# A layer with attention and experts on one core: six of nine DMA pieces of zeros in the early batch, not three, and behind the first raw weight chunk

## The reference

```python
x = x + cross_attention(_layernorm(x), ctx_768, ...)   # 16 heads of 64, its own layer norms on x and context
x = x + self_attention(_layernorm(x), W_qkv, W_o)      # 16 heads of 32, q = k = v
x = x + moe(_layernorm(x), ...)                        # 8 experts of 512 x 2048 x 512, top 2 of 8
...
logits = (x @ gate_w + gate_b) / TEMP
topk_vals, topk_idx = jax.lax.top_k(logits, TOP_K)
masked = jnp.where(keep, logits, -jnp.inf)
gate_probs = jax.nn.softmax(masked, axis=-1)
h = jax.nn.gelu(jnp.einsum('bsd,edf->bsef', x, w1) + b1, approximate=False)
expert_out = jnp.einsum('bsef,efd->bsed', h, w2) + b2
out = jnp.einsum('bse,bsed->bsd', gate_probs, expert_out)   # then a layer norm with ln_g, ln_b
```

## Time and profile before

| what | value |
|---|---|
| median of 3 runs | 1472.52 us (1472.13 to 1472.53) |
| profiled execution, its own time | 1469.05 us |
| its span, first to last instruction | 1467.4 us |
| mean granted clock of TensorE | 0.985 |
| PE busy | 1382.4 us, 94% |
| DVE, ACT, POOL busy | 53%, 40%, 11% |
| DMA | 207.52 MB, mean 141 GB/s |

### The profile page before, as it was taken

How to read it: one execution, slowest core, us unless ns; L and a number is a source line. 1 busy time by engine, 2 the same in 40 slices (tenths; PEclk the granted TensorE clock), 3 DMA queues, 4 the chain that set the end, 5 groups by cost and what they waited for, 6 DMA issues and landing times.

```text
span 1467.4 us, 24647 instructions
## 1 busy us (share of the span) xinstructions
PE 1382.4 (94%) x8042; PEld 879.9 (60%) x8043; DVE 781.0 (53%) x1871; ACT 586.5 (40%) x1082; POOL 156.8 (11%) x200
## 2 busy tenths in 40 slices
PE   6879999999999999999996899999999999999997
PEld 5658677686676876768764544444444444444442
DVE  5665876868777777787665532222222222232225
ACT  3565665756747567466670211212112121121100
POOL 1001012020020200302003100000000000000005
PEclk9999999999999999999999999999999999999997
DMA  9793142341322412325028807524325166100005
GB/s 363 269 351 144 52 154 92 116 161 50 134 102 104 182 50 109 127 79 209 29 91 329 320 28 279 217 83 158 135 105 196 44 256 249 44 21 21 14 15 172
DMA packets 53568, 207.52 MB, mean 141 GB/s; under 512 B 4902, under 2 KB 5012, under 8 KB 47388
## 3 DMA queue, kind: packets, MB, share of 16 engines
q1 hardware_dynamic: 40320, 123.14, 22.7%
q0 software_dynamic: 13184, 83.89, 14.9%
q10 hardware_dynamic: 28, 0.01, 0.0%
HBM read 144.11 MB, written 62.91 MB: 141 GB/s over the span
## 4 chain that ended last, share of the span: by engine, by line
PE 80%; DVE 8%; ACT 4%; issue 4%; POOL 2%; DMA 1%; SPq 0%; DVEq 0%; ACTq 0%; POOLq 0%
PE bank L624 22%; PE bank L1466 8%; PE bank L1424 7%; PE bank L606 6%; PE bank L608 5%; PE bank L607 5%; PE bank L1387 4%; PE bank L1492 4%; PE bank L1408 3%; PE bank L616 3%; PE bank L1433 2%; PE bank L1448 2%; PE bank L1514 2%; ACT moe_w L954 2%; DVE moe_w L1115 2%
## 5 line engine op out<-in xcount | busy, mean ns | idle before, releaser
L624 PE MATMUL bank<-moe_w,arena 128*128 x736 | 330.9, 592 | 0.0
L492 DVE SCALAR_TENSOR_TENSOR arena<-bank,now_scales,arena 128x512 f32<-128x512 f32 x92 | 69.1, 751 | 344.0 <-PE bank L608 344.0
L624 PEld LDWEIGHTS bank<-moe_w,arena 128*128 128x128 f32 x736 | 132.7, 190 | 132.5 <-issue 132.5
L1424 PE MATMUL bank<-moe_w 128*128 128x257 f32 x768 | 189.8, 385 | 6.5 <-DVE moe_w L886 6.5
L429 ACT ACTIVATE arena<-arena 128x512 f32<-128x512 f32 x92 | 58.3, 633 | 335.7 <-DVE arena L492 335.7
L1424 PEld LDWEIGHTS bank<-moe_w 128*128 128x128 f32 x768 | 138.2, 192 | 25.6 <-DVE moe_w L886 5.8
L606 PE MATMUL bank<-moe_w,arena 128*128 x368 | 139.7, 379 | 1.3 <-POOL pool_mark L384 1.3
L607 PE MATMUL bank<-moe_w,arena 128*128 x368 | 139.5, 379 | 0.0
L608 PE MATMUL bank<-moe_w,arena 128*128 x368 | 139.5, 379 | 0.0
L1466 PE MATMUL bank<-moe_w 128*128 128x512 f16 x384 | 114.4, 379 | 10.0 <-ACT moe_w L943 7.0
L929 ACT ACTIVATE moe_w<-bank,cols,ugain 128x512 f32<-128x512 f32 x96 | 74.6, 777 | 61.6 <-PE bank L1467 60.8
(11 more groups left out here) (234 smaller groups left out, 2158.4 us busy)
## 6 DMA issues: line engine op xcount, KB each, us to landing
moe_w<-w_halves POOLq DMA_DIRECT2D x8, 4096.0 KB, 13.2
moe_w<-in_L_ffn_w_dram POOLq DMA_DIRECT2D x8, 4096.0 KB, 24.4
w_halves<-moe_w SPq DMA_DIRECT2D x48, 512.0 KB, 3.1
xs_rows<-blocks SPq DMA_DIRECT2D x8, 2048.0 KB, 14.8
moe_w<-in_L_ffn_w_dram SPq DMA_DIRECT2D x16, 1024.0 KB, 6.3
arena<-in_ctx_dram SPq DMA_DIRECT2D x32, 384.0 KB
arena<-in_L_ffn_w_dram SPq DMA_DIRECT2D x8, 1024.0 KB, 4.8
blocks<-in_L_ffn_w_dram SPq DMA_DIRECT2D x8, 1024.0 KB, 4.8
```

Source lines behind the costliest of these rows:

```text
L492: nc.vector.scalar_tensor_tensor(out=h_sb[:, fb % 2, :], in0=bank[fb % 2][:, :], scalar=now_scales[:, KD:KD + 1], in1=b1_rows[:, bass.ds(s ...
L624: last = nc.tensor.matmul(Y[:, :], hT_sb[:, fb % 2, c, :], moe_flat[:, bass.ds((e % 2) * 16384 + 8192 + (4 * fb + c) * DIM, DIM)], start=( ...
L1424: last = nc.tensor.matmul(bank[h][:, 0:KEYS], qkT[:, c, b, h * P:(h + 1) * P], cnT[:, b % 2, c, :], start=(c == 0), stop=(c == KC - 1))
```

## The change

The early batch has six zeros instead of three, and the raw chunk 0 is issued ahead of it. Group 0 is handed the zeros that remain: three, all behind the first context piece. The other engines' programs are the same.

```diff
-ZERO_FIRST = 3
+ZERO_FIRST = 6
@@ in SP's program
+            sp.wait_ge(setup_full, 8)
+            raw_load(0, 0)
             sp.wait_ge(zeros_ok, 1)
             for e in range(ZERO_FIRST):
                 zero_rows(e)
-            sp.wait_ge(setup_full, 8)
-            raw_load(0, 0)
             group(0, True, range(ZERO_FIRST, EXPERTS + 1))
```

## The result

| | before | changed |
|---|---|---|
| median of 6 runs each | 1471.74 us (1469.27 to 1472.53) | 1463.83 us (1462.10 to 1465.97) |
| ratio, 95% interval | | 0.9951 (0.9939 to 0.9964) |
| profiled execution (span) | 1469.05 us (1467.4) | 1463.71 us (1462.1) |
| start of L1480 to the next group's first L1387 | 23.58 us | 17.31 us |

The changed kernel is 7.2 us faster by the ratio (5.3 to 9.0); 6.0 was forecast, and a median of 1466.5 us. The profiled execution was forecast at 1463.05 and took 1463.71. The last line of the table takes the stage round the moved wait by itself, from 97.58 to 121.16 before and from 97.22 to 114.53 after: 6.27 us less.

A forecast was written before the change was run, and what follows sets the result against it. PE, 94% busy, could gain only from idle and low clock, here its wait for the third context piece at group 0's end: 5.1 + 0.9 = 6.0 us, profiled execution 1463.05, median 1466.5 us, range 1463.0 to 1470.0.

The forecast's parts named there:

- (a): Raw chunk 0 issued ahead of the zeros: no engine waits for it, so landing earlier is worth 0 us.
- (b): Three more zeros in the early batch fill the DMA idle from 55.8 to 64.8; the sixth lands at 71.3.
- (c): First context piece, queued behind six zeros, lands at 72.1, 1.7 us before DVE's read; loss 0 to 0.4 us.
- (d): Third context piece is issued at 88.1, lands by 93.3, before DVE wants it at 96.35; 6.09 us idle goes.
- The 1.26 us of cover: First context piece's lateness hidden from PE: L1107 ends at 77.10 and PE wants its result at 78.36.
- The lower bandwidth: At 358 GB/s a 2 MiB zero takes 5.9 us; first piece 2.0 late, 0.7 lost, gain 5.3 not 6.0.
- (e): End of group 0: ACT's second row sum limits next, idle 0.30; L962 and L1492 5.1 us earlier, not 6.1.
- (f): L1492 regains 2.6 us of low clock, less 1.7 for one 3.4 us stretch: 0.9 us, bounds 0 and 2.6.
- the two outcomes: Clock falls once behind PE's remaining idle (0.9 us regained), or is spared (2.6; total 7.7, 1464.8 us, within forecast's range).
- the rival of the clock that takes back: Later 1.2 GHz stretches, up to 1.7 us each, take the gain back: 1470.8 us; chance 0.09.
- The third piece wasn't late: Rival: third context piece late all the same, SP held until 92, PE's wait stays: 1472.5 us; chance 0.07.
- The slower side: Rival: first context piece starves DVE; at 8 us per zero, 5.4 us slower, 1477.9 us; chance 0.06.

## Why the prediction was right

**(a) The chunk.** Worth 0 us, as forecast: the chunk alone gave 0.9998, and six zeros without it all of the gain.

**(b), (c), (d) The queue.** SP was free for the first piece as forecast and issued the third with its m_full. The step that was mis-sized is in (c): the first piece lands "0.8 later" than the sixth zero, at 72.1, with 1.7 to spare. In the profile it was there at 73.78, 1.2 behind the sixth zero, which itself took 6.2 us instead of 5.13 and landed at 72.6. These 1.7 us are all that was to spare. In five profiles of kernels with six early zeros DVE waited 0, 0.35, 1.86, 1.97 and 2.58 us, of which 0, 0, 0.56, 0.68 and 1.28 reached PE. The forecast's bounds of 0 and 0.4 were too narrow. The sum lacked one thing more: the time at which DVE wants the piece was read from a single execution. In the three profiles that have two stretches of low clock ahead of 60 us (the kernel before and both of the changed kernel) DVE is ready for the piece at 73.4 to 74.2; in the nine without them at 71.9 to 72.6. The waits of 1.86, 1.97 and 2.58 all belong to the nine, those of 0 and 0.35 to the three. The piece itself was there at 73.8 to 74.6 in the four profiles in which DVE waited. That the changed kernel's own profiles show next to no wait is thus partly luck. The 1.26 us of cover was right (1.30).

**The lower bandwidth.** The Trainium skill, "DMA: Bandwidth & Descriptors", Specifications, has about 358 GB/s as one core's share of the HBM. The trace does not agree: this core moved 409 GB/s over 9 us of zeros. The piece was 1.86 to 2.58 late in three profiles, but not by slower zeros: where it was 2.58 late, the six zeros landed 5.1 to 5.2 us apart.

**(e) The next wait.** Right to the tenth: ACT's idle fell to 0.30, L1500 came 2.35 after L962 and L1492 4.51 after it. Reckoned from the start of L1480, L1492 comes 8.64 after it instead of 13.72: 5.08 us, forecast 5.1.

**(f) The clock.** One stretch of 3.41 us, as taken. It gave back 1.19 us, not 0.9: at full clock L1492 has 6.98 us from its start to the next group, not 7.4. The 7.4 doubled the listed length of half of it in group 1 (3.69), and a listed length reaches past the start of the next group of matmuls: 32 in one piece are listed with 7.14, and the next group starts 6.98 after them. The clock part of the wait was thus 2.88, measured by itself with PE filled, of which the change got 1.19 and the low stretch kept 1.69 (1.7 forecast). 5.08+1.19 is the 6.27 of the stage. That the forecast took the right one of the two outcomes is luck: behind the same two idles of PE the clock fell in four profiles and didn't in three, and 1.7 us hang on it.

**The sum.** 6.3 us at the stage, 5.3 at the end of the two profiled executions, 7.2 (5.3 to 9.0) in the runs. The 1.0 between stage and end of the profiles: this start was 0.4 us earlier, and 1.3 us were lost behind the stage (1346.2 us from L1387 to the end before, 1347.6 after). Where they were lost shows at the last L593 (transposes of the rows of one of the experts' jobs), before and after:

```profile
1388.89 0.60 PE L593 MATMUL bank<-ident,arena 128*128 128x128 f32 x4
```

```profile
1382.52 0.60 PE L593 MATMUL bank<-ident,arena 128*128 128x128 f32 x4
```

Here the changed kernel is still 6.4 us ahead; 1.0 of the 1.3 is lost in what follows. There stands the last long stretch of low clock, in the kernel before

```profile
1431.26:1444.91 13.65, 13.65 (x17) 4.89 (x17) 0.58 (x1) 0.00 (x0) 8.71 (x10) 0.50 0.67 193
```

and in the changed one

```profile
1423.97:1441.04 17.07, 17.07 (x21) 6.29 (x20) 1.69 (x4) 0.00 (x0) 10.36 (x12) 0.50 0.54 155
```

This is the rival of the clock that takes back, in the size of one stretch, and all twelve profiles bear it out: from this L593 to the end it is 76.9 us with 10.2 us of long low clock (one profile), 77.8 to 78.5 with 13.7 (five), and 79.5 to 79.7 with 17.1 (six). It isn't bound to the change: the kernel with only the chunk moved, whose stage is that of before, has the 17.1, and three kernels with the third piece in time have 13.7. From L1387 to the end the twelve profiles take 1345.2 to 1348.9 us. So much does the end of one execution vary without regard to this stage, and that the profiled execution came within 0.7 us of its forecast is partly luck.

Of the 2.7 us between the forecast median of 1466.5 and the measured 1463.83, 0.8 is the kernel before itself, whose six runs have a median of 1471.74, not 1472.52. The rest lies within the interval.

**The rivals.** The third piece wasn't late. The slower side didn't come with six, but came with nine, at the place named; what made the piece late there were three more zeros ahead of it, not slower ones.

## What to carry to other kernels

When bulk transfers with no deadline share a queue with small ones that have one, list for each small one when it is wanted and how many bytes stand ahead of it, and spread the bulk so that none is late: here six of nine in front gained 7 us, nine lost 5, and in two profiles with five no piece was waited for, while with six the first one mostly was. Take the time at which a piece is wanted from several executions: here it moved by up to 2.3 us between profiles. After a wait is removed, the gain goes only as far as the next one (5.1 of 6.1 us here), and here a long idle of TensorE cost its clock on top (2.9 us for 5.9 of waiting); filling the idle with matmuls of constants got this part back without touching the wait.

## What the runs showed of the hardware

- Two stretches of low clock that both kernels' first profiles had ahead of 60 us were absent in nine of the ten later ones; the edits don't touch PE's program there. In the kernel with only the chunk moved the granted clock was 1.00 from 30 to 60, in the kernel before 0.89, and L1480 started at 95.65 and 97.58:

```profile
30.00:60.00 30.00, 22.45 (x181) 18.00 (x182) 21.66 (x59) 14.85 (x38) 2.26 (x3) 1.00 0.85 322
```

- After the same two idles of 0.78 and 1.53 us the clock fell in the stage for the changed kernel (both profiles), five early and six with the chunk behind, and didn't for three others. The same program part costs 8.67 or 6.98 us by it; differences under 2 us are not to be read from one profile. What decides between the two is open.
- Behind a full queue of 2 MiB pieces a context piece of 384 KB was there 1.2 us after the last zero in one kernel and 2.7 in another (landed at 71.9, read at 74.58); with all nine early it was 2.6 (83.2 and 85.82).
